# A message-passing layer on one core: edge attributes laid out for the first product, a row-tiled first layer, and eight of every 28 chunks summed on TensorE

## The reference

```python
h = relu(layernorm(x))                       # 6250 nodes x 128
xw = h @ W_in
W_ij = (softplus(f_ij @ W_f1 + b_f1) - ln2) @ W_f2 + b_f2     # 200000 edges, f_ij has 20 columns
x_ij = xw[dst] * (W_ij * cutoff)             # dst is sorted, src is random
s = segment_sum(x_ij, src, 6250)
out = x + (softplus(s @ W_o1 + b_o1) - ln2) @ W_o2 + b_o2
```

## Time and profile before

| | |
|---|---|
| median of 3 runs | 2643.63 us (2637.69 to 2644.58) |
| the profiled execution | 2637.52 us, its span 2635.6 us |
| busy share: PE, DVE, ACT, POOL | 89%, 70%, 65%, 73% |
| granted TensorE clock, mean | 0.968 |

### The profile page before, as it was taken

The page is one execution under the profiler, slowest core; times in us unless marked ns, Lnnn a source line. Parts: engine busy times, 40 slices in busy tenths (PEclk is TensorE's granted clock), DMA queues, the critical chain, the costliest instruction groups (busy, mean ns, idle before and its releaser), DMA issues.

```text
span 2635.6 us, 71554 instructions
## 1 busy us (share of the span) xinstructions
PE 2334.9 (89%) x19063; PEld 1729.0 (66%) x19063; DVE 1842.1 (70%) x4064; ACT 1721.8 (65%) x4279; POOL 1914.4 (73%) x1235
## 2 busy tenths in 40 slices
PE   3369999999999999999999999999999999999946
PEld 2247776776766677676676676676776676777724
DVE  7546777776777677676777777776677677777658
ACT  2147777776677677676777777677676777777713
POOL 2038887777777777877777787787777777777753
PEclk8579999999999999999999999999999999999967
DMA  7646555655655555555555555555555655555565
GB/s 261 188 78 97 91 90 88 92 87 88 91 87 87 89 90 86 88 92 86 87 88 90 86 90 90 86 88 88 89 87 88 91 87 88 88 90 88 84 140 173
DMA packets 436508, 259.95 MB, mean 99 GB/s; under 512 B 90238, under 2 KB 430181, under 8 KB 436233
## 3 DMA queue, kind: packets, MB, share of 16 engines
q0 software_dynamic: 170976, 80.61, 33.2%
q1 hardware_dynamic: 264121, 176.39, 25.0%
q10 hardware_dynamic: 1136, 0.44, 0.1%
HBM read 153.24 MB, written 104.04 MB: 98 GB/s over the span
## 4 chain that ended last, share of the span: by engine, by line
PE 59%; ACT 17%; issue 11%; DVE 4%; DMA 4%; ACTq 2%; POOL 2%; SPq 1%; DVEq 0%; POOLq 0%
PE ps L1331 13%; PE ps L1316 12%; PE ps L1288 12%; PE ps L1302 11%; PE ps L1295 6%; ACT region L721 5%; ACT region L749 5%; ACT region L719 5%; DMA acc<-region,target 2%; ACT region L732 2%; PE ps L1351 2%; PE ps L1293 1%; POOL acc L606 1%; ACTq L749 1%; ACTq L323 1%
## 5 line engine op out<-in xcount | busy, mean ns | idle before, releaser
L606 POOL DMA_INDIRECT acc<-region,target x1180 | 1863.9, 1580 | 640.1 <-issue 303.7
L1316 PE MATMUL ps<-region 128*128 128x386 bf16 x3072 | 660.9, 336 | 59.9 <-ACT region L732 46.1
L732 ACT ACTIVATE region<-ps 128x386 bf16<-128x386 f32 x768 | 372.9, 486 | 272.7 <-PE ps L1316 267.6
L1026 DVE SCALAR_TENSOR_TENSOR region<-ps,region 128x512 f32<-128x512 f32 x391 | 270.2, 691 | 375.4 <-ACT region L723 311.0
L1316 PEld LDWEIGHTS ps<-region 128*128 128x128 bf16 x3072 | 268.1, 98 | 293.7 <-ACT region L732 86.6
L749 ACT ACTIVATE region<-ps,cut_col 128x128 f32<-128x128 f32 x1564 | 442.7, 372 | 0.0
L1331 PE MATMUL ps<-region 64*128 64x392 bf16 x4608 | 418.5, 328 | 11.9 <-DVE region L1107 11.9
L1288 PE MATMUL ps<-attrT,w_f 81*128 81x128 f32 x3128 | 417.8, 276 | 12.1 <-ACT attrT L756 9.4
L1295 PEld LDWEIGHTS ps<-w_f,region 128*128 128x128 f32 x3128 | 411.3, 192 | 11.2
L1295 PE MATMUL ps<-w_f,region 128*128 128x128 f32 x3128 | 412.4, 275 | 0.0
L1288 PEld LDWEIGHTS ps<-attrT,w_f 81*128 81x128 f32 x3128 | 386.4, 192 | 27.7 <-ACT attrT L756 22.2
(11 more groups left out here) (129 smaller groups left out, 1990.7 us busy)
## 6 DMA issues: line engine op xcount, KB each, us to landing
dst_b<-dst_rows SPq DMA_DIRECT2D x391, 128.0 KB
src_b<-src_rows SPq DMA_DIRECT2D x295, 128.0 KB
xwin<-xw_parts SPq DMA_DIRECT2D x391, 63.0 KB
acc<-region,target POOLq DMA_INDIRECT x1180
attr<-in_edge_attr_dram SPq DMA_DIRECT2D x391, 40.0 KB
acc<-region SPq DMA_DIRECT2D x20, 640.0 KB, 5.1
region<-acc SPq DMA_DIRECT2D x64, 192.0 KB, 3.5
xw_parts<-parts SPq DMA_DIRECT2D x36, 256.0 KB, 3.2
```

What stands on the lines that cost most here:

```text
L606: nc.gpsimd.indirect_dma_start(out=acc[t], out_offset=bass.IndirectOffsetOnAxis(ap=target[:, slot, t:t + 1], axis=0), in_=summed[:, slot, ...
L732: nc.scalar.activation(binned[:, h, j, :], binned_ps[:, 0:PC], ACT.Copy).then_inc(s_binned, 1)
L1026: V.scalar_tensor_tensor(hidden[:, odd, :], hidden_ps, 0.0, hidden_exp[:, odd, :], ALU.max, ALU.add).then_inc(s_h, 1)
L1316: ins = MM(binned_ps[:, 0:PC], place[:, h % 2, t, j * P:(j + 1) * P], payload_high[:, h % 2, t, :], start=(t == 0), stop=(t == T - 1))
```

## The change

- The host lays out the attributes as `attr_cols`: per chunk two halves of 256 edges, each with its 20 columns as rows. SP loads the halves with two DMAs straight into `attrT`, at partitions 0 and 64. The PE transpose and the ACT copy are gone.
- `hidden_product` is two fp32 matmuls of 20 contracted rows and 256 columns, on row tiles 0 and 64, into two PSUM banks. The bias `b_f1` is given to ACT's first instruction and to `combine`.
- Three tiles' sums share bank 0; the fourth shares bank 5 with half of the hidden product. So the fourth matmul of `same_product` waits for `combine` of the chunk ahead, ACT copies the sums in two instructions (129 and 387 columns), and `hidden_product` waits for the copy of 129 columns.
- `src`, `dst` and `cutoff` come laid out in chunks and in columns; PE's and ACT's column transposes in the setup are gone, and an edge's place in its chunk is tile by tile.
- Eight of every 28 chunks are PE chunks (104 in all, 287 POOL chunks; before 96 and 295). They stand three or four steps apart. The last 27 chunks are POOL chunks (before: the last seven).
- A PE chunk's tiles are sorted 3, 3, 2 in steps n+4 to n+6 (before 1, 2, 2, 2, 1 in n+4 to n+8), and the first of a step stands ahead of the hidden product.

```diff
-U = 16
-ON_PE = (3, 7, 11, 15)
+U = 28
+ON_PE = (3, 6, 10, 13, 17, 20, 24, 27)
...
-        attrT_ps, hidden_ps = ps[0], ps[4]
-        sums_ps = ps_all[:, 0:2, P:P + 2 * FW]
-        binned_ps = ps[5]
+        hidden_ps = ps_all[:, 4:6, 0:CE // 2]
+        sums_ps = [ps[0][:, t * FW:(t + 1) * FW] for t in range(T - 1)] + [ps[5][:, CE // 2:CE // 2 + FW]]
+        binned_ps = ps[1]
...
-        BINNED_AT = {4: (0,), 5: (1, 2), 6: (3, 4), 7: (5, 6), 8: (7,)}
+        BINNED_AT = {4: (0, 1, 2), 5: (3, 4, 5), 6: (6, 7)}
         NODES_AT = ((5, 0, (3, 2)), (6, 0, (1, 0)), (7, 1, (3, 2)), (8, 1, (1, 0)))
         DENSE_AT = ((7, 0), (9, 1))
         ADDED_AT = ((8, 0), (10, 1))
...
+            def load_attr(c, slot):
+                for r in range(2):
+                    sp.dma_start(attrT[64 * r:64 * r + RBF, slot, :],
+                                 attr_cols[bass.ds(c, 1), r, :, :].rearrange("o k e -> k (o e)")).then_inc(s_attr[slot], 16)
...
-                nc.scalar.activation(a, z, ACT.Abs).then_inc(steps[0], 1)
+                nc.scalar.activation(a, z, ACT.Abs, bias=bias).then_inc(steps[0], 1)
...
+            def take_sums(slot):
+                nc.scalar.activation(summed[:, slot, T - 1, :], sums_ps[T - 1], ACT.Copy).then_inc(s_last_sum, 1)
+                nc.scalar.activation(summed[:, slot, 0:T - 1, :].rearrange("p t c -> p (t c)"), ps[0][:, 0:(T - 1) * FW], ACT.Copy).then_inc(s_s, 1)
...
-                for t in range(T):
-                    ins = MM(hidden_ps[:, t * P:(t + 1) * P], w_f1[:, t, :], attrT[0:KA + 1, odd, :], start=True, stop=True)
+                for r in range(2):
+                    rows = slice(64 * r, 64 * r + RBF)
+                    ins = MM(hidden_ps[:, r, :], w_f1[rows, :], attrT[rows, slot, :], start=True, stop=True)
                 ins.then_inc(s_hp, 1)
...
             def hybrid_products():
                 def step(u, k):
+                    jobs = binnings(u, k)
+                    for job in jobs[:1]:
+                        bin_up(*job)
                     n = k + 1
                     if exists(u, n):
-                        after(pe, s_aT, u, n)
+                        after_slot(pe, s_attr, u, n, 2)
                         after(pe, s_h, u, n - 1)
-                        hidden_product(n % 2)
-                    jobs = binnings(u, k)
-                    for job in jobs[:1]:
-                        bin_up(*job)
+                        wait(pe, s_last_sum, pool_until(u, n - 3))
+                        hidden_product(n % 4)
...
-                        if exists(u, n + 3):
-                            after(pe, s_aT, u, n + 3)
-                        same_product(n % 2)
+                        same_product(n % 2, range(T - 1))
+                        if exists(u, n + 2):
+                            after(pe, s_h, u, n + 2)
+                        same_product(n % 2, (T - 1,)).then_inc(s_sp, 1)
```

More of the change, by code:

```diff
@@ L288, in gnn_kernel, with halves @@
         quads_stored = [len(range(h, NQ, 2)) for h in range(2)]
-        ndma = sum(1 for g in range(G) if min(rows_of[g], NCH - 1 - g * P) > 0) + 1
+        def halves(columns):
+            return columns.rearrange("p (r c) -> p r c", r=2)
         def known(c):
@@ L553, in step @@
                         sp.sem_inc(s_sp_go, 1)
[L554 to L555 removed]
+                        sp.dma_start(dst_now[:, slot, :], dst_cols[:, bass.ds(c, 1), :].rearrange("p o t -> p (o t)")).then_inc(s_dnow[slot], 16)
                 general_steps(sp, step)
@@ L687, in _ @@
             nc.scalar.preload_act_table_set("natural_log_exp_and_others")
-            for j in range(2 * G):
-                column(j)
             def relu(q):
@@ L715, in _, with softplus @@
                     whole(q - 1)
-            def softplus(z, a, steps, value):
-                nc.scalar.activation(a, z, ACT.Abs).then_inc(steps[0], 1)
+            def softplus(z, bias, a, steps, value):
+                nc.scalar.activation(a, z, ACT.Abs, bias=bias).then_inc(steps[0], 1)
                 act.wait_ge(steps[0], value)
@@ L782, in step @@
                         last.then_inc(s_xg, 1)
-                    c = i + 2
-                    if there(c):
-                        past(act, s_aTp, c)
-                        past(act, s_hp, c - 2)
-                        nc.scalar.activation(attrT[0:KA, m % 2, :], attrT_ps[0:KA, 0:P], ACT.Copy).then_inc(s_aT, 1)
                     c, slot = i - 1, (m - 1) % 4
@@ L1261, in ranks @@
                 ins.then_inc(s_rkps, 1)
-            pe.wait_ge(s_w, 16 * (7 + 2 * T))
+            pe.wait_ge(s_w, 16 * 10)
             pe.wait_ge(s_shift, 1)
-            MM(ps[6][:, 0:F], ones[:, :], w_f2[:, :], start=True, stop=True)
+            MM(ps[6][:, 0:F], bf1_less_ln2[:, :], w_f2[:, :], start=True, stop=True)
             MM(ps[6][:, F:2 * F], bo1_less_ln2[:, :], w_o2[:, :], start=True, stop=True).then_inc(s_bias, 1)
-            for j in range(2 * G):
-                column(j)
             for q in range(NQ + 1):
@@ L1297, in filter_product, with same_product @@
                 ins.then_inc(s_fp, 1)
-            def same_product(odd):
-                for t in range(T):
-                    ins = MM(sums_ps[:, t // 2, t % 2 * FW:(t % 2 + 1) * FW], same[:, odd, t * P:(t + 1) * P], message[:, odd, t, :], start=True, stop=True)
-                ins.then_inc(s_sp, 1)
+            def same_product(odd, tiles):
+                for t in tiles:
+                    ins = MM(sums_ps[t], same[:, odd, t * P:(t + 1) * P], message[:, odd, t, :], start=True, stop=True)
+                return ins
             payload_high = payload.rearrange("p h t c -> p (h t c)").bitcast(bf16).rearrange(
@@ L1442, with rows, columns @@
     from concourse.bass_utils import run_bass_kernel_spmd as _run
+    src, dst = _np.asarray(inputs["src"]), _np.asarray(inputs["dst"])
+    edge_attr, cutoff = _np.asarray(inputs["edge_attr_20"]), _np.asarray(inputs["edge_weight1"])
+    edges, rbf = edge_attr.shape
+    chunks = -(-edges // CE)
+    spare = chunks * CE - edges
+    def rows(a, mode):
+        return _np.pad(a.reshape(edges), (0, spare), mode=mode).reshape(chunks, CE)
+    def columns(a):
+        return a.reshape(chunks, T, P).transpose(2, 0, 1)
+    attr = _np.pad(edge_attr, ((0, spare), (0, 0)))
+    laid = {
+        "x": _np.asarray(inputs["x"]),
+        "src": rows(src, "edge"),
+        "src_cols": columns(rows(src, "edge")),
+        "dst": rows(dst, "edge"),
+        "dst_cols": columns(rows(dst, "edge")),
+        "edge_attr_20": attr.reshape(chunks, 2, CE // 2, rbf).transpose(0, 1, 3, 2),
+        "edge_weight1": columns(rows(cutoff, "constant")),
+    }
+    for name in _WEIGHTS:
+        laid[name] = _np.asarray(inputs[name])
     nc = _bacc.Bacc("TRN2", target_bir_lowering=False, num_devices=1)
     arrays, args = {}, []
-    for name in _INS:
-        a = _np.ascontiguousarray(inputs[name])
+    for name, a in laid.items():
+        a = _np.ascontiguousarray(a)
         arrays[f"in_{name}_dram"] = a
```

208 lines of the change are left out of this document (75 added, 133 removed).

## The result

| | us | ratio to before (95%) |
|---|---|---|
| before, 4 runs | 2640.74 (2637.69 to 2644.58) | 1 |
| changed, 4 runs | 3264.53 (3245.89 to 3275.59) | 1.2354 [1.2292, 1.2416] |
| predicted | 3080 (2850 to 3240) | |

The changed kernel is slower by 624 us. The direction and the places of the waits were as predicted, the size was 185 us short, and the time lies 25 us above the range. The profiled execution took 3267.3 us, its span 3265.5, against 3072 in the sum: 193 us to account for.

The account below looks back on a forecast made before the run. Bound by a chain of waits between engines, no engine full. 143 + 52 × 50.69 (2636) − 15 + 10 + 15 + 200 + 83 = 3072 us span, 2 around it, medians 6 above: 3080, range 2850 to 3240.

Parts of the forecast that it names:

- The period of the chain: Seven loop steps, hidden product to hidden product: 6.77, 7.94, 6.77, 7.94, 6.77, 6.42, 8.08 us from step 0, sum 50.69.
- pairs: Neighbouring sorted tiles on PE share one PSUM buffer: a round trip of 1.46 us against 0.70 of issue.
- either DVE wait: PE waits for DVE's last place mask in step 2 and for its dense addition in step 6.
- the Abs with a bias tile: ACT's first instruction, at the head of every chain: the bias tile adds 0.06 us, bounds 0 and 0.06.
- Step 6: Last of the seven steps: its dense job waits for DVE's addition, PE stands from 1.29 to 3.68; 8.08 us.
- DVE's two waits don't bite: Rival: no waits for place mask (step 2) or addition (step 6), 3.70 us less per period, 2888 us; chance 0.16.
- Row tiles one behind the other: Rival: the hidden product's two row tiles run serially, 0.43 us more per step, 3237 us; chance 0.07.
- Loop turns: ten, 1.0 each: +10: Where the loop branches back: ten turns (before 21), each 1.0 us more, +10 us.
- The clock falls: Rival: step 6's wait halves PE's clock, the 4 us of work behind it double, 208 more, 3290 us; chance 0.07.
- The end: Last 27 chunks at POOL's 7.42, 200 us, beginning 15 after chunk 364's hidden product, then 83 for closing.
- The closing stage: After POOL's last DMA: 83 us as in the kernel before, bounds 75 and 95.
- step 5: Dense job, tile, sums, then the 129-column copy that the hidden product waits for; 6.42 us.

Follow-up runs that it names:

- Numbers 2: Kernel before, only the table of sorted tiles changed to 3, 3, 2 in steps n+4 to n+6: 2746.12 us, ratio 1.0401.
- Number 3: Changed kernel with DVE's dense addition moved from behind combine to the head of the step: 3091.84 us, ratio 1.1711.
- number 4: Changed kernel with DVE's dense addition and also the last place mask moved to the head of the step: 3004.18 us, ratio 1.1379.
- number 1: Changed kernel with the old tables (U = 16, four PE chunks, old five-step sorting), so the layout alone: 2694.94 us, ratio 1.0205.
- Number 7: Changed kernel with nine instead of two rounds of 28 steps written out, three rounds in the loop instead of ten: 3185.72 us, ratio 1.2077.
- number 6: As number 5, with 12 instead of 2 rounds of 16 steps written out, eleven in the loop instead of 21: 2511.86 us, ratio 0.9525.
- number 5: As number 1, with the hidden product ahead of the first sorted tile and the fourth sum done and copied first: 2509.51 us, ratio 0.9517.
- number 8: Changed kernel with addition and last mask at the head of DVE's step, first sorted tile behind hidden product, fourth sum first: 2790.64 us, ratio 1.0561.

## Why the prediction was right and wrong

- *The period of the chain.* Right: all seven steps in the predicted order and within 0.35 us, 51.49 against 50.69. Numbers 2, 3 and 4 show its parts: pairs alone bring the kernel before to 25.1 per four steps as worked out, and moving the cause of either DVE wait takes most of its time away (1.8 of 2.3 us, 1.3 of 1.3). Of the 0.8 us missing (38 us in all) the Abs with a bias tile is 0.2: it takes 0.69 where it took 0.60, and I had taken 0.06 of the 0.09. Step 6 is 8.43 instead of 8.08; DVE's combine, which the addition follows, takes 0.75 there where it took 0.69. The rest, some 0.5 per period, I did not resolve.
- *"DVE's two waits don't bite"* (2888). False as a whole: 1.31 and 2.32 us, where 1.3 and 2.4 were worked out.
- *"Row tiles one behind the other"* (3237). False: 0.70 for four records of 438 ns.
- *"Loop turns: ten, 1.0 each: +10".* This is the term that failed most. The nine turns cost 42 us themselves and 15 in the steps behind, 6.4 each, six times the row I took. I had carried the 1.0 us of the earlier trace rows over unchanged to another order of work and to a loop body that is longer, 28 steps instead of 16. The length isn't all of it: in number 1, with 16 steps, a turn costs 3.1. Number 7 confirms the size: 11.3 us per round taken out of the loop (turn, the steps behind it, and part of the long steps). In one round of the changed kernel's loop the profile has 1276 matmuls on PE, each with its weight load, before 768, and PE's gaps at the turns are of "issue"; the instruction queue q8 shows 170 packets, before 32, in number 1 29, in number 6 86, in number 7 152. That the body has become too large to be kept and is fetched anew in each round fits these numbers; it is not shown, since no run changed PE's body alone. Number 7 moves nearly as many packets as the changed kernel and is 79 us shorter, so the amount fetched is not the price.
- *"The clock falls"* (3290, given 0.07). True in part, and the second failed term: I had it as all or nothing, 208 us if step 6 throttles every time. In the loop it throttled behind 17 of 30 such waits (those at a turn and in the loop's first step not counted); all 28 long steps make 46 us, some 1.6 each, and the turns throttle besides. Number 3 shows its cause. The wait doesn't fix the rate: in the nine whole written-out rounds of number 7 that have it, 8 of 36 such steps are long. The Trainium skill (TensorE: Matmul & The Clock Gate, HAM oscillation) says that waits that recur can throttle the engine anew; the windows at 1136 to 1144 agree, with a price of 1.6 us per fall, and the trace adds that the same 2.32-us wait does so only part of the time (at 1082.45 the step took 8.42).
- *The end.* 38 us too short, since POOL's pace was taken for all of the last 27 chunks: the first dozen of them still carry the last PE chunks' sorting and dense jobs, and PE waits for DVE's masks. That was an error in reading the schedule, not in a duration. The closing stage itself was right (85 us behind POOL's last DMA).
- *What I did not see at all.* The new layout is a gain of 5% that the place of the first tile and of the fourth sum hides (number 5 against number 1: 185 us for both orders together). I had both on the chain (the tile in every step, the copy in step 5), but priced the copy at 0.37 by an xg instruction; it takes 0.28. I had not asked what the layout would be worth without them, and in number 1 forgot the tile and expected a gain.

So of the 624 us, as far as the experiments separate them: the two DVE waits and the clock falls that they cause are 260 (numbers 3 and 4), the order around the hidden product another 214 (number 8 against number 4), and 150 remain (number 8 against before), which I put down to pairs, turns and the end, less what the layout gives; these parts are not separated. The best version run, at 2509.51 us, keeps the layout, the old share of PE chunks and the old five-step sorting, and changes two orders.

Open: the cause of PE's gap at a turn (above); the share of PE chunks apart from the pairs; the two orders of number 5 apart; what a second PSUM buffer for sorted tiles would bring, which was not tried because all banks are in use; and the 24 us of small lengthening in steps inside the loop.

## What to carry to other kernels

When work goes through one buffer between two engines, two neighbours cost the whole round trip (here 1.45 us for 0.70 of issue); count how often they are neighbours before shortening the schedule. A product that everybody waits for (here the hidden one) should stand ahead of work that nobody waits for: this and the fourth sum first together turned a layout that lost 2% into one that gained 5%. A recurring wait has a second price where it lets the clock fall, and a turn of a loop has no fixed price (1.0 us before, 3.1 in number 1 with as many steps in the body, 6.4 in the changed kernel); whether either costs anything depends on who the bound is, so try the same edit in the version that you mean to keep (fewer turns: 79 us in one, nothing in the other).

## What the runs showed of the hardware that I had not expected

- The granted clock fell to one half behind the 2.32-us wait in 17 of 30 steps within the loop of one execution, and not in the other 13; each fall cost 1.6 us.
- A turn of the loop: PE 2.33 and 1.94 us of "issue" in the changed kernel, 2.61 and 3.48 in number 4, none on PE before (ACT has 2.36 us of "issue" at a turn there); ACT 3.10 us in number 1.
- Two fp32 products of 20 rows and 256 columns on row tiles 0 and 64 take 0.63 us of issue together, against 0.89 for four of 81 rows and 128 columns. Around them (1008 to 1018 in the kernel after) the weight load stands idle for 0.33 to 0.39 us ahead of its next weights, while PE's matmul rows show no gap.
- A copy of 129 columns from PSUM by ACT takes 0.28 us, of 387 columns 0.49.
